# Attention and feed-forward in one kernel: scores over all 128 rows, and the packed keys moved by ScalarE's own queue

## The reference, cut to what matters

```python
xn = layernorm(x)
qkv = einsum('bmd,ed->bme', xn, Wqkv)       # 16 heads of 16; q is scaled by 16 ** -0.5
k4, v4 = every 8th token of each segment of 512 tokens    # 64 keys a segment and head
scores = einsum('bhspd,bhskd->bhspk', q4, k4).reshape(B, H, S, nb, 64, 64)
w = exp(scores - max over the 64 queries of a block)
out = einsum(w, v4) / (sum(w over keys) + 1e-10)
attn = einsum('bmd,ed->bme', out, Wout)
ffn = relu(xn @ W1 + b1) @ W2 + b2          # 256 -> 1024 -> 256
return x + attn + ffn
```

## Time and profile before

| | |
|---|---|
| time, median of 3 runs | 1070.29 us (1067.36 to 1070.59) |
| the profiled execution | 1070.42 us, its span 1068.6 us |
| PE busy | 1046.8 us, 98% of the span |
| DVE, ACT, POOL busy | 817.3, 648.3, 622.3 us |
| DMA issued by SP | 215.96 MB, 72.5% of 16 engines' span |

### The profile page before, as it was taken

The page is one execution under the profiler, slowest core; times in us unless marked ns, Lnnn a source line. Parts: engine busy times, 40 slices in busy tenths (PEclk is TensorE's granted clock), DMA queues, the critical chain, the costliest instruction groups (busy, mean ns, idle before and its releaser), DMA issues.

```text
span 1068.6 us, 19173 instructions
## 1 busy us (share of the span) xinstructions
PE 1046.8 (98%) x5381; PEld 811.4 (76%) x5381; DVE 817.3 (76%) x1465; ACT 648.3 (61%) x1080; POOL 622.3 (58%) x487
## 2 busy tenths in 40 slices
PE   6999999999999999999999999999999999999998
PEld 4677787777787777777777877777877777877777
DVE  7877877877878777778778778778777778787753
ACT  5656665666656566565666656666666665656663
POOL 4355565656656656556655656566565565556564
PEclk9999999999999999999999999999999999999999
DMA  5457777777776878777777777778778687767744
GB/s 192 98 155 210 223 213 207 195 213 220 223 213 179 224 201 232 221 195 198 207 223 223 215 208 197 217 214 229 213 192 216 197 236 212 211 175 218 194 144 145
DMA packets 153576, 216.38 MB, mean 202 GB/s; under 512 B 27344, under 2 KB 96720, under 8 KB 153552
## 3 DMA queue, kind: packets, MB, share of 16 engines
q1 hardware_dynamic: 153408, 215.96, 72.5%
q10 hardware_dynamic: 144, 0.13, 0.0%
HBM read 100.41 MB, written 58.46 MB: 149 GB/s over the span
## 4 chain that ended last, share of the span: by engine, by line
PE 84%; DMA 6%; DVE 4%; SPq 3%; issue 2%; ACT 0%; DVEq 0%
PE h_bank L1023 36%; PE y_bank L1023 36%; PE s_banks L1096 5%; PE misc L1203 3%; PE s_banks L1203 2%; DMA k_dram<-k_lo 2%; PE misc L1023 2%; DMA yt_dram<-y_mem 1%; DVE xn L824 1%; DMA xt_dram<-z 1%; DMA k_pack<-k_dram 1%; SPq L406 1%; DVE s_max L841 1%; SPq L428 1%; DMA x_raw<-x 1%
## 5 line engine op out<-in xcount | busy, mean ns | idle before, releaser
L533 POOL TENSOR_TENSOR h_lo<-h_full,h_hi 128x512 fp32r<-128x512 f32 x256 | 336.1, 1314 | 382.2 <-ACT h_full L614 378.8
L620 ACT ACTIVATE w_exp<-w_exp 128x512 f32<-128x512 f32 x256 | 161.6, 632 | 241.8 <-DVE w_exp L847 240.2
L612 ACT ACTIVATE h_hi<-h_bank,b_cols 128x512 fp32r<-128x512 f32 x256 | 174.5, 682 | 70.2 <-PE h_bank L1023 63.4
L1023 PE MATMUL h_bank<-xt_hi,w_hi 128*128 128x512 f32 x512 | 206.4, 403 | 0.0
L1023 PE MATMUL h_bank<-xt_lo,w_hi 128*128 128x512 f32 x512 | 200.2, 391 | 0.0
L1023 PE MATMUL h_bank<-xt_hi,w_lo 128*128 128x512 f32 x512 | 199.7, 390 | 0.0
L841 DVE TENSOR_REDUCE s_max<-s_banks 128x8 f32<-128x512 f32 x254 | 170.9, 673 | 34.5 <-PE s_banks L1096 34.5
L1023 PE MATMUL y_bank<-h_hi,w_hi 128*128 128x512 f32 x496 | 194.7, 392 | 0.2 <-ACT w_exp L620 0.2
L1023 PE MATMUL y_bank<-h_lo,w_hi 128*128 128x512 f32 x496 | 193.9, 391 | 0.0
L1023 PE MATMUL y_bank<-h_hi,w_lo 128*128 128x512 f32 x496 | 193.6, 390 | 0.0
L847 DVE TENSOR_TENSOR w_exp<-s_banks,s_max 128x512 f32<-128x512 f32 x254 | 175.7, 692 | 11.0
(11 more groups left out here) (139 smaller groups left out, 1509.4 us busy)
## 6 DMA issues: line engine op xcount, KB each, us to landing
q_pack<-q_hi SPq DMA_DIRECT2D x248, 128.0 KB, 2.5
rden_rows<-rden_dram SPq DMA_DIRECT2D x128, 128.0 KB, 4.6
x_b<-x SPq DMA_DIRECT2D x32, 512.0 KB, 4.5
x_raw<-x SPq DMA_DIRECT2D x31, 512.0 KB, 4.8
q_pack<-q_lo SPq DMA_DIRECT2D x124, 128.0 KB, 2.4
yt_dram<-y_mem SPq DMA_DIRECT2D x124, 128.0 KB, 3.6
y_mem<-yt_dram SPq DMA_DIRECT2D x31, 512.0 KB, 4.7
out<-x_b SPq DMA_DIRECT2D x31, 512.0 KB, 3.1
```

The source lines that it names most:

```text
L533: pool.tensor_tensor(h_part[1][:, i % HBUF], h_full[:, i % HBUF], f32(h_part[0][:, i % HBUF]), ALU.subtract).then_inc(h_lo, 1)
L612: act.activation(h_part[0][:, i % HBUF], h_bank[i % 2][:], ACT.Relu, bias=b1_cols[:, i:i + 1]).then_inc(h_hi, 1)
L620: act.activation(w_exp[:, pair], w_exp[:, pair], ACT.Exp).then_inc(w_ready, 1)
L1023: mm = pe.matmul(ps, stationary[a], moving[b], start=start and c == 0 and n == 0, stop=stop and c == len(pairs) - 1 and n == 2, skip_group ...
```

## The change

Two things change. (1) The score matmul multiplies all 128 rows of `k_pack` and `q_pack`; POOL fills rows 96 to 127 of both with zeros at the start of the program, and the first score matmul of step 0 waits for that. (2) In each step the two transfers of the keys to DRAM and the three that pack them are issued by ScalarE, and SP no longer has them. In the lead step SP keeps them.

```diff
@@ POOL, start of the program
+            pool.wait_ge(consts_made, 3)
+            pool.memset(f32(k_pack[PR:P]).rearrange("p j c n -> p (j c n)"), 0.0).then_inc(pack_zeroed, 1)
+            pool.wait_ge(pack_zeroed, 1)
+            pool.memset(f32(q_pack[PR:P]).rearrange("p n t -> p (n t)"), 0.0).then_inc(pack_zeroed, 1)
+            pool.wait_ge(pack_zeroed, 2)
@@ SP, step
                 if norm:
-                    keys_to_dram(s)
                     pack(s, 0)
-                    pack_keys(s)
                     pack(s, 1)
@@ ScalarE, new functions
+            def key_to_dram(s, part, made):
+
+                act.wait_ge(made, s + 3)
+                act.dma_start(k_dram[part].rearrange("j d n -> (j d) n"),
+                              f32(k_part[part][:]).rearrange("p c n -> p (c n)")).then_inc(k_out, 16)
+
+            def pack_keys(s):
+
+                act.wait_ge(k_out, (s + 2) * 32)
+                for r, part in enumerate((0, 0, 1)):
+                    act.dma_start(f32(k_pack[PW * r:PW * (r + 1)]).rearrange("d j c n -> d j (c n)"),
+                                  k_dram[part].rearrange("j d n -> d j n")).then_inc(k_packed, 16)
@@ ScalarE, step
                 if norm:
-                    for m in range(DH):
-                        queries_hi(s, m)
+                    key_to_dram(s, 0, k_hi)
+                    queries_hi(s, 0)
+                    key_to_dram(s, 1, k_lo)
+                    queries_hi(s, 1)
                 if attention and ffn:
                     for quad in range(QUADS):
                         attention_hi(s, quad, par)
+                if norm:
+                    pack_keys(s)
                 if attention:
                     attention_drain(s, 0)
@@ PE, scores
-                pe.matmul(s_bank[n % 2], k_pack[0:PR, pair % (PAIRS // 2), pair // (PAIRS // 2)], q_pack[0:PR, pair], start=True,
+                if isinstance(s, int) and s == 0 and n == 0:
+                    pe.wait_ge(pack_zeroed, 2)
+                pe.matmul(s_bank[n % 2], k_pack[:, pair % (PAIRS // 2), pair // (PAIRS // 2)], q_pack[:, pair], start=True,
                           stop=True).then_inc(s_psum, 1)
```

More of the change, by code:

```diff
@@ L204, in ln_attention_ffn @@
         k_packed = sem("k_packed")
+        pack_zeroed = sem("pack_zeroed")
         v_ready = sem("v_ready")
```

## The result

The changed kernel takes 1095.79 us (median of 4 runs, 1093.02 to 1101.39) against 1069.57 us (4 runs, 1067.36 to 1070.59) for the kernel before, run beside it: a ratio of 1.0254, with a 95% interval of 1.0237 to 1.0271. It is slower by 26 us where 8 us less were forecast, and it lies above the range. The profiled execution took 1093.02 us.

What follows compares the result with a forecast made beforehand. PE, busy 1046.8 of 1068.6 us, was taken to bound the kernel. 1070.4 - 7.0 (rows) - 1.8 (key waits) + 0.3 (fills) + 0 (SP) + 0 (ScalarE) = 1061.9 us; range 1058 to 1090, the forecast's own 1058 to 1067.

Steps and rivals of the forecast that it cites:

- The score over 128 rows: PE's score matmuls: 128 rows instead of 96 remove 0.032 us a score, 7.0 us together, bounds 0 to 7.9.
- no surplus to win: Rival on PE's scores: the 0.032 us come from waits and signals, not rows; 1068.9 us, chance 0.23.
- The zero fills: POOL at program start: both fills done at 6.4 us, 0.5 ahead of the statistics; 0.3 us counted once.
- The key waits: Scores' waits for packed keys, 3.5 us in 5 places, shrink with own queues; gain 1.8 us, bounds 0 to 3.5.
- The five transfers on ScalarE at no cost: ScalarE ahead of its first num_den copy: wait and issues stay hidden in even and odd steps; 0 us.
- the landing stays long: Rival: odd key lo landing stays about 5.1 us, ScalarE's copy 1.6 us late in 15 steps; 1087 us, chance 0.15.
- issues hold each other up: Rival: ScalarE's three packs wait for SP's issues, 3.2 us instead of 1.5; 24 us, 1087 us, chance 0.19.
- a case that needed two things: The main forecast: surplus gone and ScalarE's wait and issues hidden; 1061.9 us, chance 0.41.
- the surplus: In PE's rounds: a score over 96 rows costs 0.032 us beyond a full-size matmul.
- the short landing: Odd steps' key lo transfer on ScalarE's own queue lands in 1.7 to 3.5 us instead of 5.1.

Runs made afterwards that it cites:

- experiment 9: The second run of experiment 8 with the score matmul back on 96 rows, fills kept: 1066.42 us, 0.9972 of the kernel before, against 1061.51 us with 128 rows.
- experiment 8: Experiment 3 with SP's second 512 KB load of x moved behind the second query pack: 0.9936 of the kernel before; run again, 1061.51 us, 0.9923.
- experiment 3: The changed kernel with the wait and three key packs back on SP, only the key writes to DRAM on ScalarE: 1063.39 us, 0.9934 of the kernel before.
- experiment 1: The changed kernel with all five key transfers back on SP, leaving scores over 128 rows and the zero fills: 1068.09 us, 0.9977 of the kernel before.
- experiment 11: The kernel of experiment 1 measured again: 1067.91 us, 0.9981 of the kernel before.
- experiment 2: The changed kernel with scores back on 96 rows and no fills, five key transfers on ScalarE: 1099.53 us, 1.0265 of the kernel before.
- experiment 4: The changed kernel with the wait and three key packs moved between ScalarE's two hidden tiles: 1085.39 us, 1.013 of the kernel before.
- experiment 5: The changed kernel with the two key writes to DRAM back on SP, wait and packs still on ScalarE: 1099.87 us, 1.0286 of the kernel before.
- experiment 6: The changed kernel with SP's 512 KB ahead of the keys cut to 128 KB, output partly stale: 1063.77 us, 0.9954 of the kernel before.
- experiment 10: The changed kernel with SP's 512 KB load of x moved behind the second query pack: 1071.61 us, 1.0019 of the kernel before.
- experiment 7: Experiment 1 with SP's two key writes issued ahead of the feed-forward blocks' 512 KB way back: 1063.07 us, 0.9942 of the kernel before.

## Why the prediction was wrong, point by point
**The score over 128 rows: right in kind, too large in size.** The round went from 2.975 to 2.947 where 2.94 was forecast, and the rival "no surplus to win" is refuted: experiment 9 changes the rows and nothing else, and 4.9 us go. The term was 7.0. It was 0.032 us times 217; measured, the medians of all rounds differ by 0.026, which over 217 is 5.6. The 0.032 counted all that a round takes beyond thirteen full starts; with 128 rows some 0.004 of that stay. The bounds of 0 to 7.9 held it. The rule that the rows of a weight load do not matter to its time (the Trainium skill, page "TensorE: Matmul & The Clock Gate", section "LDWEIGHTS (loading the stationary operand)") agrees with the traces as far as it goes: the loads of the scores take 188 ns in the mean with 96 rows (experiment 9) and with 128 (experiment 8). But it speaks of the load and not of the round, in which the rows of the matmul do show; so it did not make the rival right, as the prediction had it.

**The zero fills: right.** The forecast had them done at 6.4 us. POOL's timeline at the start of the changed kernel:
```profile
1.60 0.95 POOL L516 MEMSET k_pack<- 32x1024 f32 x1
2.61 3.51 POOL L518 MEMSET q_pack<- 32x4096 f32 x1
6.75 0.20 POOL L527 TENSOR_TENSOR var_eps<-mean_var,eps 128x5 f32<-128x5 f32 x1 [0.63 <-DVE mean_var L800]
```
They end at 6.12, and POOL then still waits 0.63 us for the statistics. The 0.3 us were not spent.

**The key waits: right that they shrink, and without worth.** In the changed kernel no wait for k_pack stands among the scores' waits; the wait for num_den has taken their place. With the wait back on SP, in experiment 3, they are 1.8 us (3.5 before); but the same waits with all five transfers on SP are 2.4 us in experiment 1 and 4.0 in experiment 11, so a gain from ScalarE's queue is not told from the scatter.

**The five transfers on ScalarE at no cost: the step that failed.** In the prediction's words, "Key lo on a queue of its own need not stand behind these. With a landing between the even step's 1.7 and 3.5 ...: 550.4 to 552.2". The odd landing stayed long: 5.5 in the step shown and 4.2 in the median of the 15 odd steps (5.1 before), and all 15 exceed the 3.4 us from which the prediction itself had the copy late. Over the kernels with SP's traffic ahead unchanged, the odd medians are 4.2, 4.9, 4.7 and 5.1 with the writes on ScalarE (the change, experiments 2, 3 and 4) and 5.1, 5.1, 5.3 and 5.5 on SP (before, experiments 1, 5 and 11): the queue is worth about half a microsecond, where 1.7 were needed (5.1 - 3.4). The 3.5 that the prediction took for an upper bound is the median of all 31 landings, in which the short even ones count for half; the odd ones alone, already in the trace of before, run from 3.5 to 6.0. Experiments 3 and 5 lay the loss on the wait and the packs in ScalarE's list, and 6 and 10, which keep the three issues there and shorten the landing, lay it on the wait. Experiments 6, 7 and 10 also show that the landing goes by what was asked for just ahead of it, on either queue. In medians of all steps and of the odd ones: 3.7 and 4.2 in the change, 2.3 and 2.7 behind 128 KB, 2.5 and 3.5 with the load of x moved, 1.7 and 2.3 on SP ahead of the 512 KB.
By the packet-wise turns between rings (the Trainium skill, page "DMA: Bandwidth & Descriptors", section "Queues, rings and completion order") the transfer would have passed most of SP's data; no run here shows that. The same page's section "Issuing engines are not separate DMA queues" says that transfers of all issuers run on the same 16 DMA engines and that a second issuer only saves issue time. With that the traces agree: the medians of k_lo are 3.5 on SP's and 3.7 on ScalarE's queue. Whether SP's bytes hold the DMA engines, their path to memory, or something else, no run separates.

**The rival "the landing stays long": this is what happened**, and it had 0.15. It said 1087 for a copy 1.6 us late in 15 steps. Its mechanism held; three of its sizes did not. The first scores of the odd steps are late by 21.3 - 5.3 = 16 us, not 24, since in some of the steps the landing was shorter. The even steps, counted as hidden, add 3.1: in them k_lo lands in 3.2 in the median where one row had given 1.7. One row stood for all even steps; their median in the trace of before is 2.7. And the lower clock after the longest waits, some 6.8 us, was in no case of the prediction.

**The rival "issues hold each other up": not seen.** It wanted 3.2 us for three packs beside SP's issues. They took 1.51 us in odd steps and 1.35 in even ones (medians from the trace), with SP issuing query packs in the same microseconds; SP alone took 1.27 and 1.49. No run shows the price of the lock that the Trainium skill, page "Perfetto Trace Analysis", section "DMA Instruction — HWDGE (DVE, Sync)", tells of. The only row that bore on it had shown none either, and 0.19 was too much for it.

**The chances.** 0.41 went to a case that needed two things, the surplus and the short landing; the first came true, the second rested on a rule that no row showed. The row that bore on it, the median of 3.5 over all steps, spoke for the rival, and its split by odd and even steps would have spoken more clearly.

## What to carry to other kernels
Before a transfer moves to an engine that computes, ask what that engine must wait for ahead of it: the issues were almost free here (two of them cost nothing that could be measured), the wait for a landing cost all that was queued behind it. A second queue hardly shortened a landing that was long because of bytes just asked for; moving those bytes behind it, or the small transfer ahead of them, did, on either queue. Where steps alternate, read a landing for each kind of step; a median over both hides the long ones. Where matmuls over fewer rows stand among full ones on a PE that never idles, zeroed rows are worth trying: here 4.9 us of 1066.

## What had not been expected of the hardware
After its longest waits for ScalarE, PE came back at the lower of its two clock levels. PE restarted at 302.80, 371.28, 571.37 and 704.56 us behind waits for num_den of 2.60, 2.40, 2.21 and 2.12 us, the longest of these waits, and around or just behind each restart the granted clock is at its lower level for some 3.4 us. The four stretches in the view by windows (us, then busy time of PE, PEld, DVE, ACT and POOL with instructions, granted clock, DMA share, GB/s):
```profile
302.90:306.30 3.40, 3.40 (x8) 2.67 (x9) 1.27 (x3) 0.00 (x0) 1.68 (x3) 0.51 0.35 75
371.10:374.50 3.40, 3.22 (x8) 2.58 (x9) 1.01 (x2) 0.05 (x1) 1.96 (x3) 0.50 0.26 57
572.50:575.90 3.40, 3.40 (x10) 2.63 (x9) 2.30 (x4) 0.56 (x2) 0.73 (x1) 0.50 0.61 129
705.60:709.00 3.40, 3.40 (x10) 2.63 (x9) 2.19 (x4) 0.46 (x1) 0.84 (x1) 0.50 0.59 126
```
A granted clock of 0.50 is 1.2 GHz. PE's timeline in the first of them:
```profile
304.21 0.63 PE L1044 MATMUL h_bank<-xt_lo,w_hi 128*128 128x512 f32 x1
304.64 0.63 PE L1044 MATMUL h_bank<-xt_hi,w_lo 128*128 128x512 f32 x1
305.07 0.63 PE L1044 MATMUL h_bank<-xt_hi,w_hi 128*128 128x512 f32 x1
```
The starts are 0.43 us apart instead of 0.227. Half of 4 x 3.4 us is 6.8 us of PE's time, a third of what the waits themselves cost, and more than the 5.6 that the rows give back; it is the larger part of why PE's busy time rose where a fall was forecast. In the kernel before, whose longest stop ahead of a score was 1.4 us, the trace has the lower level only behind the last matmuls. So a late copy here can cost more than its lateness: the mean granted clock was 0.999 before, 0.994 in the changed kernel and 0.984 in the profiled run of experiment 5. That the waits bring the lower level is read from their order in time; no run here sets the length of a wait by itself. Nor does the length alone decide. In experiment 2 a wait of 2.18 us that ends at 568.96 has no lower level behind it. In experiment 10 waits of 1.64 and 1.81 us, neither of them for num_den, that end at 54.55 and 955.33 have one from 55.26 and 956.38 on, and the same two waits in the changed kernel (1.64 and 1.77 us) have none. What decides between these cases no run shows.
